# V's products interleaved with the next slot's first two output products, in a cross-attention and feed-forward kernel

## What is computed

```python
# x, ctx: (32, 64, 512).  H = 32 heads, KVH = 8 key/value heads, D = 128
q = layernorm(x) @ Wq;  k = ctx @ Wk;  v = ctx @ Wv          # Wq 512x4096, Wk and Wv 512x1024
q, k = rope(q), rope(k)                                      # tables gathered by position
p = softmax(where(mask == 0, -1e9, q @ k.T / sqrt(D)))       # each k, v head serves 4 q heads
x = x + concat_heads(p @ v) @ Wo                             # Wo 4096x512
r = softmax(layernorm(x) @ gate_w.T)                         # 8 experts
x = x + ((layernorm(x) * (r @ in_scale)) @ sign(weight).T) * (r @ out_scale) + bias
```

## Time and profile before

| | us |
|---|---|
| median of 3 runs | 1149.29 (1148.65 to 1153.01) |
| the profiled execution, its own time | 1149.49 |
| its span, first to last instruction | 1147.7 |
| TensorE busy in the span | 1130.3 (98%) |
| VectorE, GpSimd, ScalarE busy | 815.5 (71%), 706.1 (62%), 537.2 (47%) |
| slot length, from scores to the next scores, slots 2 and 3 | 33.61 and 33.27 |

### The profile page before, as it was taken

How to read it: one execution, slowest core, us unless ns; L and a number is a source line. 1 busy time by engine, 2 the same in 40 slices (tenths; PEclk the granted TensorE clock), 3 DMA queues, 4 the chain that set the end, 5 groups by cost and what they waited for, 6 DMA issues and landing times.

```text
span 1147.7 us, 22887 instructions
## 1 busy us (share of the span) xinstructions
PE 1130.3 (98%) x7919; PEld 951.8 (83%) x7919; DVE 815.5 (71%) x1363; ACT 537.2 (47%) x1736; POOL 706.1 (62%) x586
## 2 busy tenths in 40 slices
PE   7999999999999999999999999999999999999998
PEld 6778888888888888888888888888888888888876
DVE  5876876767687766877767676677766767776566
ACT  4644444454444454444553435544444544445533
POOL 5855675555667556675665666566675656755544
PEclk9999999999999999999999999999999999999999
DMA  8323332333323222333422323233232232322200
GB/s 233 111 72 114 114 115 82 90 96 94 93 82 102 74 82 85 121 107 92 116 85 68 103 75 90 91 106 107 84 94 73 74 92 65 93 72 83 83 20 37
DMA packets 134339, 105.29 MB, mean 92 GB/s; under 512 B 10664, under 2 KB 108984, under 8 KB 134256
## 3 DMA queue, kind: packets, MB, share of 16 engines
q1 hardware_dynamic: 128848, 93.72, 27.8%
q10 hardware_dynamic: 4640, 8.40, 2.1%
q0 software_dynamic: 768, 2.10, 0.6%
HBM read 100.00 MB, written 4.19 MB: 91 GB/s over the span
## 4 chain that ended last, share of the span: by engine, by line
PE 91%; DVE 3%; issue 2%; DMA 1%; ACT 1%; POOL 1%; SPq 0%; DVEq 0%; ACTq 0%; POOLq 0%
PE chunk L1232 22%; PE chunk L1234 21%; PE chunk L1233 21%; PE duo_ps L1298 6%; PE o_ps L1321 3%; PE duo_ps L1221 2%; PE aux L1221 2%; PE duo_ps L1321 2%; PE chunk L1278 1%; PE o_ps L1280 1%; PE o_ps L1279 1%; PE chunk L1280 1%; PE o_ps L1278 1%; PE chunk L1279 1%; DVE swp L931 1%
## 5 line engine op out<-in xcount | busy, mean ns | idle before, releaser
L448 POOL TENSOR_TENSOR w_lo<-raw,w_hi 128x512 fp32r<-128x512 f32 x192 | 247.8, 1304 | 311.9 <-ACT w_hi L589 311.7
L931 DVE TENSOR_TENSOR swp<-chunk,sinT 64x512 f32<-64x512 f32 x320 | 220.3, 688 | 54.2 <-PE chunk L1234 33.4
L589 ACT ACTIVATE w_hi<-raw 128x512 fp32r<-128x512 f32 x192 | 116.4, 629 | 270.1 <-PE chunk L1234 203.8
L1232 PE MATMUL chunk<-xT_hi,w_hi 128*128 128x512 f32 x512 | 206.7, 404 | 0.6 <-POOL w_lo L448 0.6
L1234 PE MATMUL chunk<-xT_hi,w_lo 128*128 128x512 f32 x512 | 200.3, 391 | 0.0
L1233 PE MATMUL chunk<-xT_lo,w_hi 128*128 128x512 f32 x512 | 199.7, 390 | 0.0
L1232 PE MATMUL chunk<-wo_hi,oT_hi 128*128 128x512 f32 x496 | 196.8, 397 | 1.2 <-DVE oT_lo L865 1.2
L1234 PE MATMUL chunk<-wo_hi,oT_lo 128*128 128x512 f32 x496 | 193.5, 390 | 0.0
L1233 PE MATMUL chunk<-wo_lo,oT_hi 128*128 128x512 f32 x496 | 193.3, 390 | 0.0
L626 ACT ACTIVATE probs<-scores,neg_max 128x64 f32<-128x64 f32 x512 | 170.4, 337 | 41.2 <-DVE neg_max L887 41.2
L455 POOL TENSOR_TENSOR qT<-qT,swp 128x512 f32<-128x512 f32 x128 | 165.2, 1298 | 35.9 <-DVE qT L933 35.5
(11 more groups left out here) (271 smaller groups left out, 2033.5 us busy)
## 6 DMA issues: line engine op xcount, KB each, us to landing
raw<-in_L_xattn_Wq SPq DMA_DIRECT2D x128, 256.0 KB, 2.8
raw<-in_L_xattn_Wo SPq DMA_DIRECT2D x128, 256.0 KB, 2.7
raw<-in_L_xattn_Wk SPq DMA_DIRECT2D x32, 256.0 KB
raw<-in_L_xattn_Wv SPq DMA_DIRECT2D x32, 256.0 KB, 3.0
acc<-in_x ACTq DMA_DIRECT2D x14, 256.0 KB, 7.4
x_tile<-in_x SPq DMA_DIRECT2D x12, 256.0 KB, 2.9
c_tile<-in_ctx SPq DMA_DIRECT2D x12, 256.0 KB, 3.2
result<-y ACTq DMA_DIRECT2D x12, 256.0 KB, 2.0
```

The source lines that it names most:

```text
L448: nc.gpsimd.tensor_tensor(lo, raw[:, r, :], hi.bitcast(F32), ALU.subtract).then_inc(wsplit_lo, 1)
L589: return nc.scalar.activation(dst, src, ACT.Copy)
L931: last = nc.vector.tensor_tensor(swp[to, k, :], bank[of, :], sinT[to, here], ALU.mult)
L1232: nc.tensor.matmul(bank, a_hi, b_hi, start=i == 0, stop=False)
```

## The change

In the even slots with attention, each half of V is issued together with one output product of the following odd slot: after every two V products (256 columns) comes one output product (512 columns), 24 and 12 in all. Half 0 goes with tile 0, half 1 with tile 1. A new `v_rows_with_out` issues the waits of both parts (`v_waits`, `out_waits`) before its first product. V's halves go to `o_ps[0]` and `o_ps[1]`, and V half 0 waits for `out_lo` of tile 1 in place of `rotate` of head 3. In the odd slots the output products of tiles 0 and 1 are gone from their old places, so that tile 1's now precedes the scores. VectorE's `v_lo_split` of half 1 moves from the odd slot's start to behind `add_out(s, 1)`, and the output product of tile 1 no longer waits for `v_ok`. The first slot keeps its V (`v_rows`).

```diff
--- before.py
+++ after.py
@@ -135,7 +135,7 @@
         sc_ps, tr_ps = (duo_both[:, i, :] for i in range(2))
 
         DUO_BANK, TABLE_BANK = [sc_ps, tr_ps], o_ps[1]
-        V_BANK, FIRST_V_BANK = [chunk[1], o_ps[0]], [chunk[0], sc_ps]
+        V_BANK, FIRST_V_BANK = o_ps, [chunk[0], sc_ps]
         OUTPUTS = [o_both, duo_both]
         C_BANK, X_BANK = [aux, sc_ps, tr_ps, o_ps[0]], [chunk[2], sc_ps, aux, tr_ps]
         ROWS_BANK, SGN_BANK, GATE_BANK = [o_ps[0], o_ps[1]], [o_ps[0], sc_ps, tr_ps, aux], o_ps[1]
@@ -1043,7 +1043,6 @@
                 if s.odd:
                     even = Slot(s.q, s.g - 1, False, False, odd=0)
                     v_lo_split(even, 0)
-                    v_lo_split(even, 1)
                 if s.intake:
                     pick_positions(t[0])
                     x_stats(t[0])
@@ -1061,6 +1060,7 @@
                     x_norm(t[0])
                 if s.odd:
                     add_out(s, 1)
+                    v_lo_split(even, 1)
                 soft_b(s, 0)
                 add_out(s, 2)
                 add_out(s, 3)
@@ -1235,7 +1235,7 @@
                 return last
 
 
-            def out_proj(s, p):
+            def out_waits(s, p):
 
                 n = (s.U - 2) * PAIRS + p
 
@@ -1245,8 +1245,6 @@
                     pe.wait_ge(added, (s.U - 3) * PAIRS + (4 if p == 0 else p + 1))
                 elif p == 0:
                     pe.wait_ge(cos_done, (s.U - 1) * KQ + 3)
-                elif p == 1 and s.odd:
-                    pe.wait_ge(v_ok, s.U)
                 elif p == 1:
                     pe.wait_ge(cos_done, (s.U - 1) * KQ + 4)
                 else:
@@ -1254,34 +1252,61 @@
                 if p == 0:
                     pe.wait_ge(wsplit_lo, SLOTS * CH if s.after_last else split_count(s, -1))
                 pe.wait_ge(o_lo, n + 1)
+
+            def out_product(s, p, n):
+
+                (h, k), total = divmod(n, 3), HG * 3
                 hi, lo = (last_wo_hi, last_wo_lo) if s.after_last else (wo_hi, wo_lo)
-                split_products(chunk[OUT_BANK[p]][:, :],
-                               [(oT_hi[:, p, h, :], oT_lo[:, p, h, :], hi[:, h, :], lo[:, h, :])
-                                for h in range(HG)]).then_inc(outproj_done, 1)
-
-            def v_rows(s, i):
-
+                return nc.tensor.matmul(chunk[OUT_BANK[p]][:, :], (oT_hi, oT_hi, oT_lo)[k][:, p, h, :], (hi, lo, hi)[k][:, h, :],
+                                        start=n == 0, stop=n == total - 1)
+
+            def out_proj(s, p):
+                out_waits(s, p)
+                for n in range(HG * 3):
+                    last = out_product(s, p, n)
+                last.then_inc(outproj_done, 1)
+
+            def v_waits(s, i):
                 if i == 0:
                     pe.wait_ge(wsplit_lo, split_count(s, max(loads_of(s).index(c) for c in (V_OWN, V_NEXT))))
                     if not s.first_proj:
-                        pe.wait_ge(cos_done, s.U * KQ + 4)
+                        pe.wait_ge(o_lo, (s.U - 1) * PAIRS + 2)
                 elif s.first_proj:
                     pe.wait_ge(x_lo, 2)
-                else:
-                    pe.wait_ge(o_lo, (s.U - 1) * PAIRS + 2)
+
+            def v_product(s, i, n):
+
+                t, (c, k) = n // (3 * EC), divmod(n % (3 * EC), 3)
                 lowest = min(entry(s, V_OWN), entry(s, V_NEXT))
                 both = slice(lowest, WRING, 1 if s.first_proj else 2)
-                for t in range(2):
-                    here = span(s.side * BT + (2 * i + t) * P, P)
-                    bank = v_bank(s, i)[:, bass.ts(t, 2 * D)].rearrange("p (g d) -> p g d", g=2)
-                    for c in range(EC):
-                        nc.tensor.matmul(bank, cT_hi[:, c, here], w_hi[:, both, c, :], start=c == 0, stop=False)
-                        nc.tensor.matmul(bank, cT_hi[:, c, here], w_lo[:, both, c, :], start=False, stop=False)
-                        last = nc.tensor.matmul(bank, cT_lo[:, c, here], w_hi[:, both, c, :], start=False, stop=c == EC - 1)
+                here = span(s.side * BT + (2 * i + t) * P, P)
+                bank = v_bank(s, i)[:, bass.ts(t, 2 * D)].rearrange("p (g d) -> p g d", g=2)
+                return nc.tensor.matmul(bank, (cT_hi, cT_hi, cT_lo)[k][:, c, here], (w_hi, w_lo, w_hi)[k][:, both, c, :],
+                                        start=c == 0 and k == 0, stop=c == EC - 1 and k == 2)
+
+            def v_rows(s, i):
+                v_waits(s, i)
+                for n in range(2 * EC * 3):
+                    last = v_product(s, i, n)
                 if i == 0:
                     last.then_inc(v_half, 2)
                 else:
                     last.then_inc(proj_done, 2)
+
+            def v_rows_with_out(s, i):
+
+                odd = Slot(s.q, s.g + 1, False, False, odd=1)
+                v_waits(s, i)
+                out_waits(odd, i)
+                for n in range(2 * EC * 3):
+                    last = v_product(s, i, n)
+                    if n % 2 == 1:
+                        last_out = out_product(odd, i, n // 2)
+                if i == 0:
+                    last.then_inc(v_half, 2)
+                else:
+                    last.then_inc(proj_done, 2)
+                last_out.then_inc(outproj_done, 1)
 
             def scores_of(s, d):
                 n = (s.U - 1) * DUOS + d
@@ -1443,8 +1468,8 @@
                 if s.first_attn:
                     return first_attention(s)
                 t, f = (job and job[0] for job in jobs_of(s)[:2])
-                out_proj(s, 0)
                 if not s.odd:
+                    out_proj(s, 0)
                     out_proj(s, 1)
                 scores_of(s, 0)
                 scores_of(s, 1)
@@ -1454,8 +1479,6 @@
                     t_context(t)
                 if s.ffn:
                     t_f(f, in_slot)
-                if s.odd:
-                    out_proj(s, 1)
                 out_proj(s, 2)
                 out_proj(s, 3)
                 project(s, 0)
@@ -1482,11 +1505,11 @@
                 if s.odd:
                     project(s, 4)
                 else:
-                    v_rows(s, 0)
+                    v_rows_with_out(s, 0)
                 if s.ffn:
                     t_product(f, in_slot)
                 if not s.odd:
-                    v_rows(s, 1)
+                    v_rows_with_out(s, 1)
 
             def product_hi(f, b):
                 pe.wait_ge(osc_ok, f + 1)
```

## The result

The changed kernel takes 1251.03 us (median of 6, 1248.69 to 1254.54), the kernel before 1152.05 us in the same rounds: a ratio of 1.087 (95% interval 1.085 to 1.089). It is 8.7% slower. The direction and the first cause were forecast; the time lies 3 us above the range, and one term of the sum is to blame for nearly all of it. The profiled execution took 1251.51 us with a span of 1249.6 us, 101.9 us more than before.

The account below looks back on a forecast made before the run. The prediction took TensorE, busy nearly throughout, to bound the kernel; 1147.7 us of span + 71.8 (stops) - 1.4 (alternation) + 7 (clock) = 1225.1, or 1226.9 as profiled execution, forecast 1227 us, 6.8% slower, range 1215 to 1248.

Parts of the forecast that it names:

- The stops: Even slots: V's first product waits for GpSimd's last weight split, 42.3 us in plain and 29.4 in feed-forward slots, +71.8 us.
- The clock: After a stop TensorE's clock may drop to half; one stop in three falling, 5 x 1.5 = +7 us.
- The estimate by the rule of the Trainium skill: TensorE's clock after V's stops: all 15 would pay, an estimated 22 us instead of 7 in the sum.
- the alternation: V and output products mixed in even slots: only per-product overhead may change, -4 ns a triple, -1.4 us in all.
- the odd slots: Scores to transposed probabilities: 10.71 us remain for some 10.3 of work, so it fits; 0 us, without cover +3.
- rival D: Clock falls after nearly every stop and the odd slots' cover gives out too: 1262 us, chance 0.06.
- The bank: V half 0 waits for out_lo of tile 1, 0.29 us late, but under the stop, so it costs nothing.
- the moved split: VectorE's v_lo_split, 0.68 us, falls in the odd slot where VectorE waits for the first eight exponentials; taken as 0.
- rival B: Even slots: block 10's split comes in time, only V's new bank stops it, 6.6 us; 1154.5 us, chance 0.04.

Follow-up runs that it names:

- the wait alone: Kernel before with one line more: V's first half also waits for all eleven weight splits of its slot; 1249.86 us, ratio 1.084.
- the run with a wait for each head: Changed kernel, but each head of output product 0 waits for its own Wo block instead of one wait ahead of V; 1162.12 us, ratio 1.008.
- The run in blocks: Changed kernel with a wait per head and no alternation: V's 24 products first, then the output product's 12; 1162.82 us, ratio 1.008.
- the run that left it out: Kernel before with only V's second half alternating with output product 0, per-head waits, VectorE's order as before; 1171.07 us, ratio 1.017.

## Why the prediction was right and where it failed

*The stops: right.* Forecast 71.8 us. From the starts of V's first product and of the last product ahead of it, V is held up by 4.5 to 5.1 us in the 15 slots, 72.7 us, of which 1.4 us were there before: 71.3. Where the chain of GpSimd ends, that nothing in it can be earlier, and the count were as said, and the wait alone reproduces the loss.

*The clock: this step failed.* "I take one stop in three falling, at about half of the bound: 5 x 1.5 = +7 us". The number of falls was three times that, 15 of 15, and the price of one was 1.3 to 2.7 us, 2.0 in the mean. Between V's start and the scores the changed kernel spends 212.4 us in the 15 slots, the run with a wait for each head 182.9 us at the full clock: 29.5 us. Of the 22.5 us that were missing 15 are the count (10 falls more, at 1.5 us) and 7 the price. The two rows I interpolated between, no fall after 2.4 us of waiting in the prologue and the slow start, could not say how near 4.5 us is to either; "a wait of that size costs nothing" was one of two outcomes, and the rarer one, since the same wait ended in a fall in 10 of 12 profiles. The estimate by the rule of the Trainium skill (TensorE: Matmul & The Clock Gate, HAM oscillation), all 15 stops at 22 us, was the better one, and I should have given it the greater chance, as that section, too, is about a wait in every round of a loop. The range did reach to "ten to fifteen stops at some 2 us", but put 28 us for them where fifteen make 30, and that on top of -1.4 us for the alternation. So what came, a fall after every stop with the odd slots still covered, lies just above its top; rival D had the falls, but tied them to a loss of that cover which did not come.

*The alternation: its sign was wrong, on a small term.* Forecast -1.4 us, at 463 ns a triple; measured +1.4, at 468: in the run with a wait for each head the 15 slots gain 42.3 us between V's start and the scores over the kernel before (182.9 against 140.6), and lose 40.9 us in the odd slots, out of which one output product went. The run in blocks gives +1.0, so this is the price of the new place, not of the alternation, which is zero.

*The bank, the odd slots, the moved split.* The bank is hidden under the wait, as said; without that cover it costs 6.6 us, as rival B had it, though by luck: B had 0.44 us in each of the 15 slots, measured are 0.33 in the 9 plain and 0.59 in the 6 feed-forward ones. The odd slots stay clear. The moved split costs nothing, but "nothing" hid what it does: in the run that left it out 6 slots waited 2.4 us each.

*The sum.* 1226.9 + 22.5 (clock) + 2.8 (alternation) - 0.5 (stops) = 1251.7, against 1251.5 us of the profiled execution.

## What to carry to other kernels

A function that takes over two pieces of work also takes over the later of their waits; put each wait just before the first instruction that needs it, and read off the releasing engine's timeline when that is. When TensorE is the bound, cost a stop of some microseconds as the stop plus the slow products after it (here 4.8 + 2.0 us each), and take the fall of the clock as likely unless several rows of that rest length show otherwise; one row is not enough. Two product sizes that carried the same overhead per product gained nothing here by being mixed.

## What was not expected of the hardware

The fall of the clock has no sharp edge in the length of the rest: 3 of 6 rests of 2.4 us, 4 of 9 of 2.5 to 2.7 us, 13 of 15 of 3.1 to 3.2 us (in two runs), and 30 of 30 of 4.4 us and more ended in it; at the end of the kernel even 2 of 12 of 1.4 us did. At the lower clock the products stand exactly 213 and 427 ns apart, without the 13 to 14 ns that each carries at the full one (120 and 227 ns). Filling a rest with idle products is worth real time (26 us here for 240 products) where the rest itself can't be avoided.
